# Third layer norm split into two halves with banks of its own, and reordered engine lists for Mamba

## The reference

```python
def _layernorm(x):                       # no weights
    return (x - mean(x)) / sqrt(var(x) + 1e-5)

def _mamba(x):                           # run forward and on the flipped sequence
    xp, z = split(x @ W_in.T)            # 256 channels each
    xc = silu(causal_conv4(xp) + b_conv)
    dt, B, C = split(xc @ W_x.T)
    dt = softplus(dt @ W_dt.T + b_dt)
    # 16 states per channel, scanned along the sequence:
    h = h * exp(dt * A) + (dt * xc) * B;  y = sum_n h * C
    return ((y + xc * D) * silu(z)) @ W_out.T

x = x + attn_block(_layernorm(x))        # layer norm again, then 0.5 * (mamba fwd + mamba bwd) + residual
x = x + transformer(_layernorm(x))       # the third norm feeds 6 layers of local attention and gated feed-forward
```

## Time and profile before

| what | value |
|---|---|
| time, median of 3 runs | 3966.04 us (3959.29 to 3967.46) |
| profiled execution, device time | 3973.11 us |
| its span, first to last instruction | 3971.3 us |
| mean granted TensorE clock | 0.964 of full speed |
| busy in the span: PE, DVE, POOL, ACT | 94%, 84%, 81%, 73% |

### The profile page before, as it was taken

One profiled execution on the slowest core, in us unless ns is written; L12 is line 12 of the kernel. 1 busy time (PEld: TensorE's weight loads), 2 busy tenths in 40 slices (PEclk: granted clock), 3 DMA queues, 4 the chain that ended last, 5 costly groups with the idle time before them and its releaser, 6 DMA issues.

```text
span 3971.3 us, 110564 instructions
## 1 busy us (share of the span) xinstructions
PE 3732.7 (94%) x43392; PEld 2529.3 (64%) x43392; DVE 3320.7 (84%) x3407; ACT 2912.0 (73%) x6890; POOL 3235.6 (81%) x2370
## 2 busy tenths in 40 slices
PE   7999999997579999999999999999999999999997
PEld 2333333333267777777777777777777777777775
DVE  4999999999478887888878888788878888788885
ACT  6555545553268887888878888788878888788885
POOL 3888788888388888888888888888888888888883
PEclk8999998899789999999999999999999999999999
DMA  1222222222100000000000000000000000000001
GB/s 66 79 70 71 77 70 70 75 73 82 46 5 13 2 16 2 17 2 16 2 2 17 2 16 2 6 13 2 16 2 6 13 2 16 2 6 2 2 2 44
DMA packets 30703, 102.12 MB, mean 26 GB/s; under 512 B 4580, under 2 KB 6504, under 8 KB 29296
## 3 DMA queue, kind: packets, MB, share of 16 engines
q1 hardware_dynamic: 30192, 95.05, 7.0%
HBM read 90.32 MB, written 4.72 MB: 24 GB/s over the span
## 4 chain that ended last, share of the span: by engine, by line
PE 67%; issue 2%; ACT 1%; POOL 1%; DVE 0%; POOLq 0%; ACTq 0%; DVEq 0%
PE ps L1101 17%; PE ps L1029 13%; PE ps L1090 9%; PE ps L1040 8%; PE ps L1078 7%; PE ps L1126 5%; PE ps L1139 3%; PE ps L1063 1%; PE ps L1051 1%; PE ps L1108 1%; PE ps L1114 1%; ACT prob L1232 0%; PE ps L1011 0%; ACT mixed L1241 0%; POOL resid L1530 0%
## 5 line engine op out<-in xcount | busy, mean ns | idle before, releaser
L1508 POOL TENSOR_TENSOR resid<-resid,sq 128x1024 f32<-128x1024 f32 x384 | 910.3, 2376 | 3.9 <-DVE sq L1362 3.7
L626 POOL TENSOR_TENSOR read<-state,c_row 128x1024 f32<-128x1024 f32 x256 | 714.9, 2811 | 165.6 <-DVE state L588 85.7
L1530 POOL TENSOR_TENSOR resid<-resid,rnorm 128x1024 f32<-128x1024 f32 x384 | 725.0, 1904 | 18.1 <-POOL rnorm L1522 0.4
L1101 PE MATMUL ps<-mixed,w_vo 128*128 128x128 f32 x6144 | 720.2, 276 | 3.0 <-ACT mixed L1241 2.3
L1101 PEld LDWEIGHTS ps<-mixed,w_vo 128*128 128x128 f32 x6144 | 711.1, 192 | 13.0 <-issue 4.6
L1029 PE MATMUL ps<-w_qk,xs_parts 128*128 128x512 f32 x2304 | 640.3, 414 | 43.6 <-issue 18.7
L1232 ACT ACTIVATE prob<-ps,stat 128x64 f32<-128x64 f32 x3072 | 650.9, 383 | 0.3
L1362 DVE TENSOR_TENSOR sq<-ps,rope_l 128x1024 f32<-128x1024 f32 x384 | 462.5, 1205 | 104.7 <-ACT sq L1194 104.7
L393 PE MATMUL mamba_ps<-read,ident 128*128 128x512 f32 x1024 | 520.8, 652 | 14.8 <-POOL read L626 14.8
L1375 DVE TENSOR_TENSOR resid<-ps,rope_l 128x1024 f32<-128x1024 f32 x384 | 464.4, 1209 | 69.4 <-ACT sq L1194 62.3
L1029 PEld LDWEIGHTS ps<-w_qk,xs_parts 128*128 128x128 f32 x2304 | 415.8, 192 | 157.9 <-issue 81.7
(11 more groups left out here) (138 smaller groups left out, 5685.9 us busy)
## 6 DMA issues: line engine op xcount, KB each, us to landing
c_row<-c_rows SPq DMA_DIRECT2D x128, 512.0 KB, 3.6
w_stage<-w_qk_hbm SPq DMA_DIRECT2D x6, 1024.0 KB, 4.8
vo_stage<-w_v_hbm SPq DMA_DIRECT2D x6, 512.0 KB, 3.8
vo_stage<-w_o_hbm SPq DMA_DIRECT2D x6, 512.0 KB, 4.6
xn<-x_hbm SPq DMA_DIRECT2D x4, 512.0 KB, 7.0
kept<-resid SPq DMA_DIRECT2D x8, 256.0 KB, 4.5
resid<-kept SPq DMA_DIRECT2D x8, 256.0 KB, 4.4
out_hbm<-resid SPq DMA_DIRECT2D x8, 256.0 KB, 2.0
```

Source lines behind the costliest of these rows:

```text
L626: pool.tensor_tensor(read[:, h, g % 2, :], state[:, h, g % 2, :], c_row[:, g % C_AHEAD, :], ALU.mult).then_inc(done[f"rd{h}"], 1)
L1101: last = pe.matmul(bank[:, 0:P], w_vo[:, l % 2, head_at(place_h), :], mixed[:, odd, place_h, :], start=place_h == 0, stop=place_h == HEADS ...
L1508: pool.tensor_tensor(qk[:, tile % 2, cols], qk[:, tile % 2, cols], sq[:, 1 + part, :], ALU.add).then_inc(done[f"rotated{part}"], 1)
L1530: pool.tensor_tensor(heads, heads, norms, ALU.mult).then_inc(done[f"normed{part}"], 1)
```

## The change

It has two parts.

**Third norm.** The centred values no longer take turn banks. Chunks 0 to 3 use banks 0 to 3 of `ps`; chunks 4 to 7 use banks 2 and 3 in alternation. PE centres four chunks before the first variance. Chunks 4 to 7 move behind work of the first two tiles: the centring of 4 and 5 behind `project0` of tile 0, their variances behind `project1` of tile 0, their squares ahead of `square0`, their logarithms and exponentials between `square0` and `square1`, their products on DVE behind `cosines0`; chunks 6 and 7 follow the same way one stage later. `project0` of tile 0 waits for two finished chunks (banks 0 and 1), the first score for all eight. The weight splits on ACT follow chunk 3, the folds follow the last variance. The number of instructions stays the same.

**Mamba's lists.** All five lists and the lists of the first norms are written anew. Each period holds the same entries; what follows is the order within it, beside the part that stays.

```diff
 # MAMBA_PE, around states 12 to 16
-(2, 12, "b"), (2, 10, "y1"), (1, None, "dt11"), (2, 13, "b"), (0, None, "x11"), (0, None, "x01"), (2, 11, "y0"),
-(2, 14, "b"), (2, 11, "y1"), (2, 12, "y0"), (2, 13, "y0"), (2, 15, "b"), (2, 12, "y1"), (2, 13, "y1"), (2, 14, "y0"),
+(1, 12, "b"), (0, None, "dt11"), (1, 10, "y1"), (2, 13, "b"), (0, None, "x11"), (0, None, "x01"), (2, 11, "y0"),
+(2, 14, "b"), (2, 11, "y1"), (2, 12, "y1"), (2, 12, "y0"), (2, 15, "b"), (2, 13, "y1"), (2, 13, "y0"), (2, 14, "y1"),
 # MAMBA_PE, around states 7 to 10
-(2, 4, "y1"), (2, 7, "b"), (2, 4, "y0"), (1, None, "dt01"), (2, 5, "y0"), (1, None, "z10"), (2, 5, "y1"), (2, 8, "b"),
-(1, None, "dt00"), (1, None, "dt10"), (2, 6, "y0"), (2, 6, "y1"), (2, 9, "b"), (2, 7, "y1"), (2, 7, "y0"), (2, 10, "b"),
+(1, 4, "y1"), (1, 7, "b"), (0, None, "z11"), (0, None, "dt01"), (0, None, "dt00"), (1, 4, "y0"), (1, 5, "y0"),
+(1, 8, "b"), (0, None, "dt10"), (1, 6, "y0"), (0, None, "z10"), (1, 9, "b"), (1, 5, "y1"), (1, 7, "y0"),
+(1, 6, "y1"), (1, 10, "b"), (1, 8, "y0"), (1, 7, "y1"), (1, 9, "y0"), (1, 11, "b"),
 # MAMBA_ACT
-(1, None, "ln1"), (2, 14, "dec0"), (0, None, "ax01"), (0, None, "ax11"), (2, 15, "dec0"),
+(1, None, "ln1"), (2, 14, "dec1"), (2, 14, "dec0"), (2, 15, "dec0"), (0, None, "ax11"), (0, None, "ax01"),
 # MAMBA_DVE
-(1, 12, "sc1"), (0, None, "split"), (1, 13, "dr0"), (1, 13, "dr1"), (1, 12, "sc0"), (1, 13, "sc0"), (1, 13, "sc1"), (1, 14, "dr0"),
+(1, 12, "sc1"), (1, 12, "sc0"), (1, 13, "dr0"), (1, 13, "dr1"), (1, 13, "sc1"), (1, 13, "sc0"), (0, None, "split"), (1, 14, "dr0"),
 # MAMBA_POOL: ar0 one product earlier, tx0 two later, ar1 ahead of both products of state 14
 # MAMBA_SP: cst from behind cd 13 to behind cd 7
 # start of the kernel, PE list as unrolled
-... bc1:0 bc0:0 z11:0 dt01:0 nm:7 nv:6 z10:0 dt00:0 dt10:0 nv:7 dt11:0 x11:1 x01:1 b:0
+... bc0:0 bc1:0 z11:0 dt01:0 dt00:0 dt10:0 z10:0 nm:7 nv:6 dt11:0 x11:1 nv:7 x01:1 b:0

-    pe[0:0] = staggered(("in_centre", 0), ("in_variance", 1)) + [("fold0", 0), ("fold1", 0)]
-    act_in = staggered(("in_square", 0), ("in_log", 1), ("in_rstd", 1))
-    insert_after(act_in, ("in_rstd", 3), ("high_qk0", 0))
-    insert_after(act_in, ("in_rstd", 5), ("high_qk1", 0))
-    act[0:0] = act_in + [("copy_folded0", 0), ("copy_folded1", 0)]
-    dve[0:0] = [("in_norm", c) for c in range(CHUNKS)]
+    def norms(*stages):
+        return [(f"in_{name}", c) for name, c in stages]
+
+    pe[0:0] = norms(*[("centre", c) for c in range(4)], *[("variance", c) for c in range(4)])
+    act[0:0] = norms(("square", 0), ("square", 1), ("log", 0), ("rstd", 0), ("square", 2), ("log", 1), ("rstd", 1), ("square", 3),
+                     ("log", 2), ("rstd", 2), ("log", 3), ("rstd", 3)) + [("high_qk0", 0), ("high_qk1", 0)]
+    dve[0:0] = norms(*[("norm", c) for c in range(4)])
+    for first, places in ((4, (("project0", 0), ("round", 0), ("project1", 0), ("square0", 0), ("cosines0", 0))),
+                          (6, (("in_variance", 5), ("square1", 0), ("project0", 1), ("square0", 1), ("sines1", 0)))):
+        two = (first, first + 1)
+        insert_after(pe, places[0], *norms(*[("centre", c) for c in two]))
+        insert_after(act, places[1], *norms(*[("square", c) for c in two]))
+        insert_after(pe, places[2], *norms(*[("variance", c) for c in two]))
+        insert_after(act, places[3], *norms(*[(name, c) for c in two for name in ("log", "rstd")]))
+        insert_after(dve, places[4], *norms(*[("norm", c) for c in two]))
+    insert_after(pe, ("in_variance", 7), ("fold0", 0), ("fold1", 0))
+    insert_after(act, ("in_rstd", 7), ("copy_folded0", 0), ("copy_folded1", 0))
...
+    def in_bank(chunk):
+
+        return ps[:, chunk if chunk < 4 else S + chunk % 2, :]
...
             def in_centre(chunk):
-                bank = turn_free("in_centre", chunk)
-                pe.matmul(bank, centring[:, :], ...
+                if chunk >= 4:
+                    pe.wait_ge(x_ready, chunk - 1)
+                pe.matmul(in_bank(chunk), centring[:, :], ...
...
+                    if tile == 0:                  # in project
+                        pe.wait_ge(x_ready, 2)
...
+                    pe.wait_ge(x_ready, CHUNKS)    # in score, tile 0
```

More of the change, by code:

```diff
@@ L33 @@
 MAMBA_PE = [
[9 rows of a table removed]
-MAMBA_ACT = [
[10 rows of a table removed]
-MAMBA_DVE = [
[10 rows of a table removed]
-MAMBA_POOL = [
[6 rows of a table removed]
[9 rows of a table added]
+MAMBA_ACT = [
[10 rows of a table added]
+MAMBA_DVE = [
[10 rows of a table added]
+MAMBA_POOL = [
[6 rows of a table added]
 MAMBA_SP = [
-    (1, 2, "cd"), (1, 3, "cd"), (1, 4, "cd"), (1, 5, "cd"), (1, 6, "cd"), (1, 7, "cd"), (1, 8, "cd"), (1, 9, "cd"),
-    (1, 10, "cd"), (1, 11, "cd"), (1, 12, "cd"), (1, 13, "cd"), (0, None, "cst"), (1, 14, "cd"), (1, 15, "cd"),
-    (0, 0, "cd"), (0, 1, "cd")]
+    (0, None, "cst"), (1, 8, "cd"), (1, 9, "cd"), (1, 10, "cd"), (1, 11, "cd"), (1, 12, "cd"), (1, 13, "cd"),
+    (1, 14, "cd"), (1, 15, "cd"), (0, 0, "cd"), (0, 1, "cd"), (0, 2, "cd"), (0, 3, "cd"), (0, 4, "cd"), (0, 5, "cd"),
+    (0, 6, "cd"), (0, 7, "cd")]
 DRIVE_IN_PSUM = (4, 9, 10, 11, 14, 15,)
@@ L80 @@
     (0, "nm", 0), (0, "nm", 1), (0, "nv", 0), (0, "nv", 1), (0, "nm", 2), (0, "nm", 3), (0, "nv", 2), (0, "nm", 4),
-    (1, "nv", 3), (2, "nm", 5), (2, "nv", 4), (4, "nm", 6), (4, "nv", 5), (10, "nm", 7), (10, "nv", 6), (13, "nv", 7)]
+    (1, "nv", 3), (2, "nm", 5), (2, "nv", 4), (4, "nm", 6), (4, "nv", 5), (13, "nm", 7), (13, "nv", 6), (15, "nv", 7)]
 FRONT_ACT = [
@@ L93 @@
     (0, "prep_nega", 0), (0, "nw", 2), (0, "nn", 2), (0, "nu", 2), (0, "nw", 3), (0, "nn", 3), (0, "nu", 3),
[2 rows of a table removed]
[2 rows of a table added]
 FRONT_POOL = [
-    (0, "nr", 0), (0, "nr", 1), (0, "nr", 2), (0, "nr", 3), (0, "nr", 4), (0, "nr", 5), (2, "nr", 6), (4, "nr", 7)]
+    (0, "nr", 0), (0, "nr", 1), (0, "nr", 2), (0, "nr", 3), (0, "nr", 4), (2, "nr", 5), (3, "nr", 6), (4, "nr", 7)]
 MAMBA_EXPS = ("nl", "ne", "nh", "ng", "nf", "prep_a", "dec0", "dec1", "ex0", "ex1", "ln0", "ln1")
@@ L746 @@
 FOLD_AFTER, FOLD_COPIED_AT = "mean", ("round", 10)
-TURN_READERS = {"in_centre": "in_norm", "in_variance": "in_log",
+TURN_READERS = {"in_variance": "in_log",
                 "head_turn0": "copy_heads0", "head_turn1": "copy_heads1", "head_turn2": "copy_heads2",
@@ L773, in insert_after @@
     seq[k:k] = stages
-def staggered(*stages):
-    return [(name, i - behind) for i in range(CHUNKS + 1) for name, behind in stages if 0 <= i - behind < CHUNKS]
 def engine_sequences():
@@ L980, in in_centre @@
             def in_centre(chunk):
-                bank = turn_free("in_centre", chunk)
-                pe.matmul(bank, centring[:, :], resid[:, chunk * BANK:(chunk + 1) * BANK], start=True, stop=True
+                if chunk >= 4:
+                    pe.wait_ge(x_ready, chunk - 1)
+                pe.matmul(in_bank(chunk), centring[:, :], resid[:, chunk * BANK:(chunk + 1) * BANK], start=True, stop=True
                           ).then_inc(done["in_centre"], 1)
@@ L993, in turn_free @@
                     ff_added(pe, CHUNKS + last[1])
-                elif last and last[0] == "in_centre":
-                    pe.wait_ge(x_ready, last[1] + 1)
                 elif last and last[0] in ("fold0", "fold1"):
@@ L1288, in in_square @@
                 after(act, ("in_centre", chunk))
-                act.activation(in_work(chunk), turn_bank("in_centre", chunk), ACT.Square).then_inc(done["in_square"], 1)
+                act.activation(in_work(chunk), in_bank(chunk), ACT.Square).then_inc(done["in_square"], 1)
             def in_log(chunk):
@@ L1327, in in_norm @@
                 for to, rows_h, ready in ((low, slice(0, 64), x_low), (high, slice(64, 128), x_ready)):
-                    dve.tensor_tensor(to, turn_bank("in_centre", chunk)[rows_h], in_work(chunk)[rows_h], ALU.mult).then_inc(ready, 1)
+                    dve.tensor_tensor(to, in_bank(chunk)[rows_h], in_work(chunk)[rows_h], ALU.mult).then_inc(ready, 1)
             def table(part, i, tile):
```

## The result

| what | before | after |
|---|---|---|
| time, median | 3966.22 us (3959.29 to 3967.46) | 3931.50 us (3928.81 to 3938.00) |
| ratio | | 0.9922, 95% interval 0.9908 to 0.9935 |
| profiled execution, and its span | 3973.1, 3971.3 us | 3938.0, 3936.2 us |
| mean granted TensorE clock | 0.964 | 0.975 |
| first scan product (`dr0`) | 77.52 us | 77.92 us |

The change gains 34.7 us between the medians, and 31 us (26 to 36) by the ratio; 32 were forecast. In this pair of profiles 20.2 us come before the third norm and 15.0 behind it, and nothing from the start. How far that split can be trusted is a question of its own, taken up with the experiments.

The account below looks back on a forecast made before the run. PE bounds the layers, DVE the scans, and chains of waits between engines the other three stretches. Gains of 18 + 11 + 3.6 = 32.6 us take the median from 3966.0 to 3934 us, range 3914 to 3956.

Parts of the forecast that it names:

- The third norm (18 us): Third norm and first tiles: an earlier tile 0, less longer projection intervals, gains 18 us, between 10 and 27.
- The walk at the low clock: Third norm: `project0` 32.9 us earlier, intervals giving back 17.9, so `project1` of tile 1 comes 15.0 us earlier.
- the bound of 31: First tiles: ACT's `square0` later than 31 us after the third norm's first centring would show the forecast wrong.
- The lead "lasts to the end": Layers behind `project1` of tile 1: lists and PE's work unchanged, so the lead gained by then stays whole.
- Mamba, steady state (11 us): Scans: `dt11` ahead of a read-out shortens DVE's wait at state 14; 11 us gained, between 7 and 20.
- Mamba, start (3.6 us): Start of the scans: x11 goes earlier and the first scan starts 3.6 us earlier, between 0 and 6.
- which allows x11 at about 60.5 us: Start of the scans: ACT reaches z10's copy about 18 us of its own work after z01's, freeing x11's bank.
- The first (clock up in both stretches, 3917): Rival: full clock in third norm and scans, 49 us gained, 3917 us; chance 0.13.
- The second (the scans gain nothing): Rival: state 14's wait is PE's matmuls, not their start; only 18 us remain, 3948 us; chance 0.17.
- The third (the norm gives back what it takes): Rival: tile 0 starts early but later intervals stretch; 3 us there, 11 in Mamba, 3952 us; chance 0.08.
- The fourth (late read-outs stop DVE): Rival: in the scans late read-outs delay POOL's products and so DVE; slower, some 3975 us; chance 0.04.
- Costed at nothing: Moves of `cst`, `tx0`, `ar0`, `sz0` and `sz1` on SP, ACT and POOL: covered by slack or idle time, 0 us.

Follow-up runs that it names:

- e1_norm: The kernel before with the new third norm alone, Mamba's and the first norms' lists as before: 0.9948 of before.
- e5_back: The changed kernel with one swap in PE's list undone, `dt11` behind the read-out `y1` of state 10 again: 0.9946 of before.
- e10_front: The changed kernel with ACT's stages of chunks 6 and 7 of the first norms moved behind the softplus of the first sequence: 0.9926 of before.
- e12_after: The changed kernel once more, unaltered, on the chip of the three runs beside it: 0.9926 of before.
- e8_way: The changed kernel with the third norm's chunks 4 to 7 giving way to the tiles' own squares and sums: 0.9885 of before.
- e3_dt11: The kernel before with one swap in PE's list, `dt11` ahead of the read-out `y1` of state 10: 0.9959 of before.
- e6_apart: The changed kernel with all eight chunks of the third norm ahead of tile 0, nothing between the first projections: 0.9925 of before.
- e2_lists: The kernel before with the new lists of Mamba and the first norms alone, third norm as before: 0.9968 of before.
- e9_both: The changed kernel with e8_way's edit and POOL's rest of tile 0 ahead of the second weight split: 0.9880 of before.
- e11_all: The changed kernel with both edits of e9_both and that of e10_front: 0.9866 of before, median 3909.3 us.

## Why the prediction was right, and where its steps were not

**The third norm (18 us): right.** The walk at the low clock held place by place. `project0` of tile 0 was put 23 us behind the first centring and stands at 21.3 to 22.3 us in the five executions with this norm; the intervals were put at 11.1, 15.7 and 11.8 us and are 10.19, 15.15 and 10.99; `project1` of tile 1 was put at 58 to 61 us and stands at 58.2, in the other four at 56.1 to 57.6. `square0` came 28.4 us after the first centring, under the bound of 31. From the first centring to the end, the profiled executions with the old norm take 2942.2 us in the mean of four, those with the new one as it was changed 2924.4 in the mean of five (2920.0 to 2927.0; after, e1_norm, e5_back, e10_front, e12_after): 17.8 us. The timed share is 21, with 18 inside its interval. The walk itself gave 15.0 us and 3 were added for the clock. In the first execution tile 0 came 0.9 us earlier than walked and the intervals were 2.3 us shorter, with the projections still at 2.90 us.

**The lead "lasts to the end": nearly.** The lead of 18.2 us at `project1` of tile 1 is 15.0 at the end in the first pair. Behind that point the layers take 2865.5 us in before, 2863.2 in e1_norm, 2868.8 and 2868.7 in the two of after and 2869.6 in e8_way, in the same order of instructions but for e8_way, where chunks 6 and 7 and the folds still follow. What moves these few microseconds was not found.

**Mamba, steady state (11 us): the place and the cause right, a little small in size.** The forecast weighed a wait shorter by 1.4 us, if the matmuls kept their 9.90, against one gone whole at 7.0, and took 2 us for each of five sequences. The runs decided for the second: 7.13 and 7.14 us, no wait. With 3.3 for each of five and 1.2 for the first the step gives 17.7 us; in the old list the swap measured 16, in the new one 10, and all the lists, whose start gave nothing, 13. The term that was a little small is the 2 us for each sequence, nearer to the first case than to the second. It counted the earlier start and only in part that the read-out, moved into the gap, takes away PE's idleness, and that where the clock falls all the same it falls on the read-out (3.54 us), which DVE isn't waiting for.

**Mamba, start (3.6 us): wrong.** It gained nothing (77.92 against 77.52 us). The step that failed is "which allows x11 at about 60.5 us". ACT's copies of z00 and z01 in the kernel before, and then in the changed kernel the same copies, that of z10, and the relu of `dt10`:

```profile
41.82 1.07 ACT L471 COPY zs<-mamba_ps 128x512 f32<-128x512 f32 x2
...
43.74 1.07 ACT L471 COPY zs<-mamba_ps 128x512 f32<-128x512 f32 x2
60.02 0.60 ACT L433 ACTIVATE resid<-mamba_ps 128x512 f32<-128x512 f32 x1 [1.61 <-PE mamba_ps L305]
63.38 0.57 ACT L471 COPY zs<-mamba_ps 128x512 f32<-128x512 f32 x1
63.84 0.69 ACT L497 ACTIVATE dtx<-mamba_ps,packed 128x512 f32<-128x512 f32 x1
```

The copy of z01 comes 1.9 us later than before, and that of z10 19.1 us behind it where 18 were counted, so it begins at 63.38 us and not at 60.4. ACT's waits for PE in between come to 4.7 us, so the 18 us were not "its own work". The other half is a wait that the step left out: `dt11` stands ahead of x11 in PE's list and waits for the relu of `dt10`, which ACT does behind z10's copy. With `dt11` from 64.68 us, x11 follows at 66.65.

And e10_front shows that the step had a second fault: even an x11 at 61.78 us does not start the scans earlier, because the norm's last variance stands in PE's list before x01, PE idles for it, and x01 then runs at the low clock.

**The sum.** Measured by parts, 21 and 13 stand for 18 and 14.6. Within the second the misses cancel, which is luck: the steady state was some 2 us too small and the start 3.6 too large.

**The rivals.** The first (clock up in both stretches, 3917) was half right: the clock is up while x11 and x01 run, and not in the third norm, where the first tiles' projections still take 2.90 us. The Trainium skill, TensorE: Matmul & The Clock Gate, section on what is actually happening, says that being busy releases the array's clock. e8_way agrees in kind: projections of 1.64 us at a granted clock of 0.92, with PE busy for 25.3 of 35 us against 20.4 at 0.74. Putting norm chunks between the tiles didn't do that by itself; removing the waits did. The second (the scans gain nothing) is refuted by e3_dt11 and e5_back. The third (the norm gives back what it takes) fails as a whole, but its mechanism is real for the interleaving: e6_apart starts tile 0 15.4 us later and loses nothing. The fourth (late read-outs stop DVE) did not happen: DVE never waits for `read`, and POOL's 256 products take 2772 ns in the mean, as against 2811 before. POOL itself does wait longer for read-outs, 94.1 us in all against 78.1, without a wait of DVE behind it. Nor did overlaps of the two engines' work cost DVE more than before: it is busy for 897.6 us in the scans against 896.2.

**Costed at nothing.** `cst`, `tx0`, `ar0`, `sz0` and `sz1` left no wait on DVE, and the lists as a whole are worth what their one swap is. (`ar0` stands three products earlier than before, not one as the section on the change has it.)

## To carry over

Look for an instruction that can stand in the gap between a write and its late reader on the engine whose clock matters: exchanging two neighbours gave 16 us of 3965, because the idleness went and the slow stretch of the clock no longer fell on work that DVE waits for. When work is put among other work, let the chain that ends last go first and the filler second; the same stages in the other order cost 15 us. And sum an engine's walk with its waits, and check what stands in the lists ahead of the sped-up instruction, and between it and the one that is waited for.

## What the runs showed of the hardware

- With the old order of the two neighbours (four executions, six sequences each) PE idles for 2.55 or 2.83 us shortly before the sixteen matmuls, and they take 8.51 to 9.90 us. With the new order (ten executions) no idleness just before them is longer than 1.5 us, and they take 7.13 to 7.17 us in 59 of 60 sequences and 9.13 us in one. I had held both possible but leant to the long one.
- The fall of the clock isn't always gone with the idleness: in the fourth sequence of the changed kernel it lies on the four matmuls of the read-out, 3.54 us at a granted clock of 0.54 instead of 1.98.
- One and the same list ran its scans in 951.8 and 940.5 us in two executions. With the idleness at state 13 gone, ten executions lie within 6 us. That the new order is steadier isn't shown: the old one has two executions, and the timed runs of e2_lists spread over 14.6 us, those of before beside them over 17.3.
- In the first tiles the six matmuls of a projection take 2.90 us or 1.64 us. With the waits of the second to fourth projection cut from 4.42, 5.10 and 2.94 us to 0.87, 3.13 and none, all three went from the one to the other in e8_way; with the same order in e9_both and e11_all one of them still took 2.59 and 2.90 us.
